# Attention masks kept in SBUF for all heads instead of being loaded for every score step

## The chip, the cores and the metric

One Trainium2 chip, all 8 NeuronCores, one launch, no exchange between the cores. The metric is the device time in microseconds of the slowest core.

## The reference, cut to what matters

One transformer layer: x is [2, 4096, 2048]; causal attention with 16 query heads and 4 key/value heads of 128, then a feed-forward part with LoRA experts.

```python
x = x + attn(_layernorm(x))        # scores = q k^T / sqrt(128); masked where key > query; softmax; @ v; @ wo
x = x + ffn(_layernorm(x))         # silu(x W1) * (x W3) with rank-32 experts, top 2 of 8, then W2
```

## The kernel before

Each core owns 1024 query rows of one sequence. It works in four stages, each engine's instructions being queued in program order, with semaphores between the engines.

Stage A (L255 to L413) normalises the sequence of 4096 rows and the core's own 1024 in tiles of 256, and projects K and V, which stay in SBUF. Then a short pass squares K (into `sq_t`) and finds its largest norm on the DVE (L411 to L453).

Stage C goes over the 16 heads (L465 to L652). A head starts with its Q projection (32 matmuls, L473), then a norm bound for the softmax (L488 to L536, small operations on four engines in turn). Then come 32 steps over blocks of 128 keys. Step `sx` emits its scores, `emit_sc`, and behind them `emit_lav` of step `sx-2` (row sums by a column of ones, L598 and L601, and the product with V, L606 and L609). Steps 0 to 15 serve both halves of the queries (7 matmuls of 512 columns with those of `emit_lav`), steps 16 to 31 only the second (4 matmuls). The causal mask is added on TensorE: a matmul of -60 times the identity with a 128x512 mask tile (L556 in the first half, L566 in the second). ACT takes the exponentials (L582, L586). A head ends with two reciprocals, their broadcast (L632, L634) and the scaling of its output.

The mask tile of step `sx` lies in one of two buffers, `mk_sb[sx % 2]`, and is loaded anew in every step of every head, by the sync engine's queue. That queue waits until the scores of step `sx-2` are done, since they read the same buffer:

```python
P.wait('sync', 'pe', scg_s.get(sx - 2) or scg31_prev)
mdma = P.dma('sync', mk_sb[sx % 2], masks_h[:, sx * 512:(sx + 1) * 512], sem=f'dM{sx % 2}')
```

The score matmuls of step `sx` wait for it, in front of the first of them (L553 or L563), besides the exponential that frees their PSUM bank.

The output projection follows (16 tiles `oc`, L669): `wo_sb` by the GpSimd queue, after the last head, and the residual `xoc_sb` by the sync queue, in front of a DVE addition (L680); then two stores. `xoc_sb[0]` waits for nothing but the mask loads queued ahead of it. The feed-forward part D follows in two halves of 512 rows.

The areas of the stages overlap in SBUF: the working area of stage C starts where that of stage A starts, and `sq_t` of stage A ends up under `wo_sb`, `xoc_sb` and `ev_sb` of the output projection.

Of the kernel before, what the change touches and what calls it, by code (L numbers as in the profile page):

```python
# [11 lines left out]
BF16 = mybir.dt.bfloat16  # L12
# [84 lines left out]
def build_program():  # L97
    nc = bass.Bass('TRN2', target_bir_lowering=False)

    def din(name, shape, dtype=F32):  # L100
        return nc.dram_tensor(name, list(shape), dtype, kind='ExternalInput').ap()
# [12 lines left out]
    masks_h = din('masks_h', [128, 32 * 512], BF16)  # L114
# [27 lines left out]
    with es:  # L142
# [17 lines left out]
        WC = Arena(nc, SB_WORK, SB_GLB, 'wc')  # L160
# [5 lines left out]
        mk_sb = [WC.al(f'mk{i}', [128, 512], BF16) for i in range(2)]  # L166
        recA = WC.al('recA', [1, 512], F32)
        recB = WC.al('recB', [1, 512], F32)
        wo_sb = [WC.al(f'wo{i}', [128, NCH * 128], BF16) for i in range(2)]
        xoc_sb = [WC.al(f'xoc{i}', [128, TOWN], F32) for i in range(2)]  # L170
        ev_sb = [WC.al(f'ev{i}', [128, TOWN], F32) for i in range(2)]

        WD = Arena(nc, SB_WORK, SB_GLB, 'wd')
        w13 = [WD.al(f'w13_{i}', [128, 2 * NCH * 128], BF16) for i in range(2)]
# [31 lines left out]
        nbi_sb = GLB.al('nbi', [128, 128], BF16)  # L206
# [22 lines left out]
        P = _P(sems)  # L229
# [25 lines left out]
        for i in range(NT + 2):  # L255
# [12 lines left out]
            if have:  # L268
                lnb = pb[4 + (i % 2)]
                wts = [(f'dX{i % 2}', ms['xb'][i]), ('dC1', d_c1)]  # L270
# [10 lines left out]
            if 0 <= j < NT:  # L281
                lnb = pb[4 + (j % 2)]
                wts = [('pe', ms['sumsq'][j])]
# [21 lines left out]
            if have:  # L305
                wts = [(f'dX{i % 2}', ms['xb'][i])]
# [14 lines left out]
            if 0 <= j < NT:  # L321
                bcb = pb[6 + (j % 2)]
                wts = [('ve', ms['post'][j])]
# [20 lines left out]
            if 0 <= j < NT:  # L344
# [4 lines left out]
                wts = [('ve', ms['rbb'][j])]  # L349
# [21 lines left out]
            if 0 <= jj < NTA:  # L371
# [19 lines left out]
                wts = [('ve', ms['ap'][jj]), ('dWkv', d_wkv)]  # L391
# [20 lines left out]
        a_pe, a_sc, a_ve = P.cnt['pe'], P.cnt['sc'], P.cnt['ve']  # L412
# [38 lines left out]
            ], waits=[('ve', kb_ve)], inc='ve')  # L451
        kb_done = kb_ve
        kb_pe_done = kb_pe_last  # L453

        P.wait('gpsimd', 've', a_ve)
        P.wait('gpsimd', 'pe', a_pe)
# [2 lines left out]
        scg31_prev = None  # L459
# [3 lines left out]
        for h in range(NH):  # L463
# [15 lines left out]
            wts = [(f'dQ{h % 2}', qdma)]  # L479
# [57 lines left out]
            exp_s, lav_s, scg_s = {}, {}, {}  # L537

            def emit_sc(sx):
                rot = sx % 2  # L540
                pi = sx % 4
                bA = pb[2] if rot == 0 else pb[0]
                bB = (pb[3] if rot == 0 else pb[1]) if sx < 16 else pb[sx % 4]
                ksl = slice(kv * S + sx * 128, kv * S + (sx + 1) * 128)
                if h == 0 and sx == 0:
                    P.wait('sync', 've', a_ve)
                    P.wait('sync', 'pe', a_pe)
                P.wait('sync', 'pe', scg_s.get(sx - 2) or scg31_prev)
                mdma = P.dma('sync', mk_sb[sx % 2], masks_h[:, sx * 512:(sx + 1) * 512],
                             sem=f'dM{sx % 2}')  # L550
                scms = []
                if sx < 16:
                    scms.append((lambda ksl=ksl, h=h, bA=bA: (lambda e: e.matmul(  # L553
                        bA[:, 0:512], K_sb[:, ksl], q_sb[h % 2][:, 0:512],
                        start=True, stop=False, skip_group_check=True)))())
                    scms.append((lambda sx=sx, bA=bA: (lambda e: e.matmul(  # L556
                        bA[:, 0:512], nbi_sb, mk_sb[sx % 2],
                        start=False, stop=True, skip_group_check=True)))())
                    scms.append((lambda ksl=ksl, h=h, bB=bB: (lambda e: e.matmul(  # L559
                        bB[:, 0:512], K_sb[:, ksl], q_sb[h % 2][:, 512:1024],  # L560
                        start=True, stop=True, skip_group_check=True)))())
                else:
                    scms.append((lambda ksl=ksl, h=h, bB=bB: (lambda e: e.matmul(  # L563
                        bB[:, 0:512], K_sb[:, ksl], q_sb[h % 2][:, 512:1024],
                        start=True, stop=False, skip_group_check=True)))())
                    scms.append((lambda sx=sx, bB=bB: (lambda e: e.matmul(  # L566
                        bB[:, 0:512], nbi_sb, mk_sb[sx % 2],
                        start=False, stop=True, skip_group_check=True)))())
                wts = [(f'dM{sx % 2}', mdma)]
                if sx <= 1:  # L570
                    wts += [('ve', qev), ('ve', vnbc)]
                elif sx < 16:
                    wts.append(('sc', exp_s[sx - 2]))
                elif sx < 20:
                    wts.append(('sc', exp_s[15]))
                else:
                    wts.append(('sc', exp_s[sx - 4]))
                scg_s[sx] = P.g('tensor', scms, waits=wts, inc='pe')

                exps = []  # L580
                if sx < 16:
                    exps.append((lambda rot=rot, pi=pi: (lambda e: e.activation(  # L582
                        out=p_sb[pi][:, 0:1024], in_=pq[1 - rot][:, 0:1024], func=AF.Exp,
                        bias=sml[:, 0:1])))())
                else:
                    exps.append((lambda pi=pi, bB=bB: (lambda e: e.activation(  # L586
                        out=p_sb[pi][:, 512:1024], in_=bB[:, 0:512], func=AF.Exp,
                        bias=sml[:, 0:1])))())
                pv = lav_s.get(sx - 4) or lav_prev4.get(sx - 4 + 32)
                exp_s[sx] = P.g('scalar', exps,  # L590
                                waits=[('pe', scg_s[sx]), ('ve', vnbc)] + ([('pe', pv)] if pv else []),
                                inc='sc')
# [24 lines left out]
            for sx in range(32):  # L617
                emit_sc(sx)
                if sx >= 2:
                    emit_lav(sx - 2)  # L620
# [27 lines left out]
            scg31_prev = scg_s[31]  # L648
            lav_prev4 = {k: lav_s[k] for k in (28, 29, 30, 31)}

        c_heads_pe = P.cnt['pe']
# [3 lines left out]
        for oc in range(NCH):  # L655
            if oc < 2:
                P.wait('gpsimd', 'pe', c_heads_pe)
            else:
                P.wait('gpsimd', 've', oc_ve[oc - 2])
            wodma = P.dma('gpsimd', wo_sb[oc % 2], wo_h[oc], sem=f'dO{oc % 2}')  # L660
            if oc >= 2:
                P.wait('sync', 've', oc_ve[oc - 2])
            xocdma = P.dma('sync', xoc_sb[oc % 2], xo_oc[oc], sem=f'dXoc{oc % 2}')

            oms = []
            for half in range(2):
                for hc2 in range(NCH):
                    def mk_o(half=half, hc2=hc2, oc=oc):
                        return lambda e: e.matmul(  # L669
                            pb[2 * (oc % 2) + half][:, 0:512],  # L670
                            wo_sb[oc % 2][:, hc2 * 128:(hc2 + 1) * 128],
                            acat[:, hc2 * TOWN + half * 512: hc2 * TOWN + (half + 1) * 512],
                            start=(hc2 == 0), stop=(hc2 == NCH - 1), skip_group_check=True)
                    oms.append(mk_o())
            wts = [(f'dO{oc % 2}', wodma), ('ve', evac_prev)]
            if oc >= 2:
                wts.append(('ve', oc_ve[oc - 2]))
            pe_oc = P.g('tensor', oms, waits=wts, inc='pe')
            oc_ve[oc] = P.g('vector', [
                (lambda half, oc=oc: (lambda e: e.scalar_tensor_tensor(  # L680
                    ev_sb[oc % 2][:, half * 512:(half + 1) * 512],
                    pb[2 * (oc % 2) + half][:, 0:512], bo_sb[:, oc:oc + 1],
                    xoc_sb[oc % 2][:, half * 512:(half + 1) * 512],
                    op0=ALU.add, op1=ALU.add)))(half)
                for half in range(2)
            ], waits=[('pe', pe_oc), (f'dXoc{oc % 2}', xocdma),
                      (f'dSt{oc % 2}', oc_st[oc - 2] if oc >= 2 else 0)], inc='ve')
            P.wait('sync', 've', oc_ve[oc])
            for tt in range(2):
                v = P.dma('sync', xres_d[tt, :, oc, :], ev_sb[oc % 2][:, tt * TD:(tt + 1) * TD],  # L690
                          sem=f'dSt{oc % 2}')
            oc_st[oc] = v
# [10 lines left out]
        for tt in range(2):  # L703
            P.wait('sync', 'dSt0', xres_st0)
            P.wait('sync', 'dSt1', xres_st1)
            if prev_dn_ve:
                P.wait('sync', 've', prev_dn_ve)
            xr_dma = P.dma('sync', xrt.rearrange('p (c n) -> p c n', c=NCH), xres_d[tt],
                           sem='dXr')
# [24 lines left out]
            wts = [('ve', vcast)]  # L734
# [95 lines left out]
            for ts in range(4):  # L830
# [12 lines left out]
                wts = [('dXr', xr_dma), ('ve', dnm), ('ve', dse_v)]  # L843
# [76 lines left out]
            for mi, dstbuf in ((0, mer[0]), (1, mer[1]), (2, wmer[0]), (3, wmer[1])):  # L920
                for eh in range(2):
                    wts = [('ve', ts_ve)]
# [207 lines left out]
            for hc in range(NCH):  # L1130
                qpe = None
                for q in range(4):
# [17 lines left out]
                    wts = [(('dW0', 'dW1', 'dW2')[idx % 3], w2dma), ('ve', x2ve[NFC - 1])]  # L1150
                    if q == 0 and hc >= 2:
# [8 lines left out]
                wts = [('pe', pedn), ('dXr', xr_dma),  # L1160
                       (f'oS{hc % 2}', last_st[hc % 2])]
# [130 lines left out]
```

How the kernel before makes its waits and increments, by code:

```python
        def run(e, dst=dst, src=src, s=s):  # L69
            e.dma_start(out=dst, in_=src).then_inc(s, 16)
# [3 lines left out]
    def wait(self, eng, sem, v):  # L74
        if not v:
            return
        s = self.sems[sem]
        self.streams[eng].append(lambda e, s=s, v=v: e.wait_ge(s, v))
# [6 lines left out]
        def run(e, builders=tuple(builders), ws=ws, inc=inc, incn=incn):  # L85
            for sname, v in ws:
                e.wait_ge(sems[sname], v)
            last = None
            for f in builders:
                last = f(e)
            if inc is not None:
                last.then_inc(sems[inc], incn)
# [1081 lines left out]
        @blk.sync  # L1174
        def _(e):
            for f in P.streams['sync']:
                f(e)
            e.wait_ge(sems['oS0'], n_out0)
            e.wait_ge(sems['oS1'], n_out1)
```

## Time and profile before

| what | value |
|---|---|
| median of 3 runs | 4073.96 us (4065.46 to 4077.08) |
| the profiled execution's own time | 4082.54 us |
| its span on the slowest core, core 4 | 4080.5 us |
| spans of the 8 cores | 4044.1 to 4080.5 us |
| TensorE busy, share of the span | 80% |
| head 8 on core 4, Q projection to the next head's | 81.9 us |
| mask loads | 512 of 128 KB |

The profile is of one execution. Rows name engine, line, operation and tiles: PE is TensorE, SPq the sync engine's DMA queue, POOL GpSimd. The ends of matmuls are modelled: in a dense stream they start 0.21 to 0.22 us apart while each is shown with 0.38 us, so an idle gap as the profile gives it is shorter than the time lost between the starts.

### The profile page before, as it was taken

The numbers are of one execution on the slowest core, as the hardware profiler recorded it, in microseconds if no ns is written. First come the engines' busy times: TensorE is split into PE (matmuls) and PEld (weight loads), VectorE is DVE, ScalarE is ACT, GpSimd is POOL, SyncE is SP. The second block draws the span as 40 slices with busy tenths as digits, with TensorE's granted clock in tenths as the row PEclk, the third lists the DMA queues.
The fourth block names the chain that finished last, engine by engine and source line by source line (L and its number), as shares of the span: only waits on it lengthen the run. The fifth ranks groups of instructions, "written<-read, shape, count | busy, mean of one in ns | idle before, by whom it ended". The sixth has DMA issues, their size and how long they took to land.

```text
span 4080.5 us, 39777 instructions; the slowest of 8 cores (4044.1 to 4080.5 us)
## 1 busy us (share of the span) xinstructions
PE 3257.8 (80%) x13863; PEld 1386.0 (34%) x14108; DVE 840.0 (21%) x1355; ACT 732.3 (18%) x882; POOL 292.5 (7%) x556
## 2 busy tenths in 40 slices
PE   5887737777777778777745999998894599999898
PEld 3454412222222222222314444443331344444333
DVE  2333341111111211111122122222001222222200
ACT  1111124333343334332000101110000001111000
POOL 0000000000000000000000111111110011111111
PEclk7778858888888888888975999999997599999999
DMA  5121212221222122212650777665894166666588
GB/s 97 31 42 32 42 30 60 63 58 49 59 59 64 51 56 62 61 49 57 164 138 9 116 122 122 119 122 93 139 154 97 26 122 124 121 121 118 95 150 142
DMA packets 166528, 350.15 MB, mean 86 GB/s; under 512 B 19259, under 2 KB 99396, under 8 KB 162500
## 3 DMA queue, kind: packets, MB, share of 16 engines
q0 software_dynamic: 79488, 246.45, 35.8%
q1 hardware_dynamic: 86852, 101.15, 8.0%
q8 instruction: 123, 2.02, 0.2%
q14 instruction: 65, 0.53, 0.0%
HBM read 577.17 MB, written 16.78 MB: 146 GB/s over the span
## 4 chain that ended last, share of the span: by engine, by line
PE 66%; DMA 15%; DVE 10%; issue 4%; ACT 4%; another core or an unknown queue 0%; SPq 0%; DVEq 0%; ACTq 0%; POOL 0%; POOLq 0%
PE pq L991 9%; PE pq L1002 9%; PE pq L1145 5%; DMA wd_w2s<-w_h 5%; DMA wc_mk<-masks_h 3%; PE pq L376 3%; PE pq L473 3%; PE pq L385 3%; DMA wc_xoc<-xo_oc 2%; PE pq L609 2%; PE pq L601 2%; PE pq L598 2%; PE pq L606 2%; PE pq L563 2%; PE pq L553 2%
## 5 line engine op out<-in xcount | busy, mean ns | idle before, releaser
L1145 PE MATMUL pq<-dp_x2s,wd_w2s 128*128 128x512 bf16 x1756 | 403.2, 382 | 60.1 <-DMA wd_w2s<-w_h 57.4
L991 PE MATMUL pq<-wd_xln,wd_w 128*128 128x512 bf16 x1756 | 407.7, 383 | 45.0 <-DMA wd_b<-b_h 39.5
L1002 PE MATMUL pq<-wd_xln,wd_w 128*128 128x512 bf16 x1752 | 402.0, 379 | 2.1
L582 ACT ACTIVATE wc_p<-pq,gl_sml 128x1024 bf16<-128x1024 f32 x256 | 284.9, 1113 | 216.6 <-PE pq L559 214.8
L1145 PEld LDWEIGHTS pq<-dp_x2s,wd_w2s 128*128 128x128 bf16 x1792 | 171.4, 98 | 288.9 <-issue 98.0
L991 PEld LDWEIGHTS pq<-wd_xln,wd_w 128*128 128x128 bf16 x1792 | 176.2, 99 | 260.2 <-issue 54.1
L1043 ACT ACTIVATE dp_s<-pq 128x512 bf16<-128x512 f32 x112 | 66.9, 597 | 1031.8 <-PE pq L1036 1009.7
L1070 DVE TENSOR_TENSOR dp_x<-dp_s,pq 128x512 bf16<-128x512 bf16 x112 | 77.1, 688 | 835.5 <-PE pq L1062 827.7
L1002 PEld LDWEIGHTS pq<-wd_xln,wd_w 128*128 128x128 bf16 x1792 | 175.4, 98 | 211.4
L625 DVE RECIPROCAL wc_recA<-pq 1x512 f32<-1x512 f32 x16 | 53.5, 3346 | 886.8 <-PE pq L609 886.8
L586 ACT ACTIVATE wc_p<-pq,gl_sml 128x512 bf16<-128x512 f32 x256 | 175.9, 687 | 212.3 <-PE pq L566 204.4
L70 POOL DMA_DIRECT2D wd_w<-w_h x224 | 118.9, 537 | 1202.1 <-PE pq L1005 878.9
L601 PE MATMUL pq<-wc_p,gl_ocb 128*1 128x512 bf16 x512 | 197.2, 385 | 1.2
L609 PE MATMUL pq<-wc_p,pp_V 128*128 128x512 bf16 x491 | 192.7, 393 | 2.9 <-issue 2.4
L669 PE MATMUL pq<-pp_acat,wc_wo 128*128 128x512 bf16 x502 | 123.4, 406 | 40.0 <-DMA wc_wo<-wo_h 39.5
L563 PE MATMUL pq<-wc_q,pp_K 128*128 128x512 bf16 x252 | 94.9, 377 | 72.5 <-DMA wc_mk<-masks_h 41.2
L473 PE MATMUL pq<-pp_xlnown,wc_wq 128*128 128x512 bf16 x501 | 142.4, 451 | 5.8 <-DVE gl_cms L450 4.8
L553 PE MATMUL pq<-wc_q,pp_K 128*128 128x512 bf16 x253 | 108.6, 429 | 25.8 <-DMA wc_mk<-masks_h 17.7
L376 PE MATMUL pq<-wa_xln,wkv_wk 128*128 128x256 bf16 x1024 | 128.6, 292 | 0.0
L632 PE MATMUL pq<-wc_recA,gl_orf 1*128 1x512 f32 x32 | 32.6, 1121 | 115.1 <-DVE wc_recB L628 115.1
L385 PE MATMUL pq<-wkv_wv,wa_xln 128*128 128x512 bf16 x496 | 117.8, 399 | 1.1
L376 PEld LDWEIGHTS pq<-wa_xln,wkv_wk 128*128 128x128 bf16 x1024 | 105.7, 105 | 24.9 <-issue 6.7
(180 smaller groups left out, 3360.0 us busy)
## 6 DMA issues: line engine op xcount, KB each, us to landing
wd_w<-w_h POOLq DMA_DIRECT2D x224, 512.0 KB, 7.3
wc_mk<-masks_h SPq DMA_DIRECT2D x512, 128.0 KB, 2.0
wd_w2s<-w_h POOLq DMA_DIRECT2D x128, 448.0 KB, 6.3
wa_xb<-x_tiles POOLq DMA_DIRECT2D x16, 1024.0 KB, 9.2
wd_b<-b_h POOLq DMA_DIRECT2D x112, 128.0 KB, 7.6
wc_wq<-wq_h POOLq DMA_DIRECT2D x16, 512.0 KB, 5.3
wc_xoc<-xo_oc SPq DMA_DIRECT2D x16, 512.0 KB, 7.1
wc_wo<-wo_h POOLq DMA_DIRECT2D x16, 512.0 KB, 7.4
```

The source lines that it names most:

```text
L376: return lambda e: e.matmul(pb[kv // 2][:, (kv % 2) * TA:(kv % 2 + 1) * TA], wk_sb[:, hc * 512 + kv * 128: hc * 512 + (kv + 1) * 128], xln ...
L385: return lambda e: e.matmul(pb[2 + sub][:, 0:512], xln_t[jj % 2][:, hc * TA + sub * 128: hc * TA + (sub + 1) * 128], wv_sb[:, hc * 512:(hc ...
L473: return lambda e: e.matmul(pq[0][:, half * 512:(half + 1) * 512], wq_sb[h % 2][:, hc * 128:(hc + 1) * 128], xlnown[:, hc * TOWN + half * ...
L553: scms.append((lambda ksl=ksl, h=h, bA=bA: (lambda e: e.matmul(bA[:, 0:512], K_sb[:, ksl], q_sb[h % 2][:, 0:512], start=True, stop=False, ...
L563: scms.append((lambda ksl=ksl, h=h, bB=bB: (lambda e: e.matmul(bB[:, 0:512], K_sb[:, ksl], q_sb[h % 2][:, 512:1024], start=True, stop=Fals ...
L582: exps.append((lambda rot=rot, pi=pi: (lambda e: e.activation(out=p_sb[pi][:, 0:1024], in_=pq[1 - rot][:, 0:1024], func=AF.Exp, bias=sml[: ...
L586: exps.append((lambda pi=pi, bB=bB: (lambda e: e.activation(out=p_sb[pi][:, 512:1024], in_=bB[:, 0:512], func=AF.Exp, bias=sml[:, 0:1])))())
L601: lav.append((lambda pi=pi, sx=sx: (lambda e: e.matmul(pb[5][0:1, 0:512], ocb_sb, p_sb[pi][:, 512:1024], start=(sx == 0), stop=(sx == 31), ...
L609: lav.append((lambda pi=pi, vsl=vsl, sx=sx: (lambda e: e.matmul(pb[7][:, 0:512], V_sb[:, vsl], p_sb[pi][:, 512:1024], start=(sx == 0), sto ...
L991: x1ms = [(lambda hc, bx1=bx1, w=lw13: (lambda e: e.matmul(bx1[:, 0:TD], w(hc, 0), xln2[:, hc * TD:(hc + 1) * TD], start=(hc == 0), stop=F ...
L1002: x3ms = [(lambda hc, bx3=bx3, w=lw13: (lambda e: e.matmul(bx3[:, 0:TD], w(hc, 1), xln2[:, hc * TD:(hc + 1) * TD], start=(hc == 0), stop=F ...
L1145: return lambda e: e.matmul(pb[hc % 2][:, 0:TD], w2s[idx % 3][:, jj * 128:(jj + 1) * 128], x2s[:, fc2 * TD:(fc2 + 1) * TD], start=(q == 0 ...
```

## The change

All 32 mask tiles are loaded once, as one tensor `mkall` of 128 x 16384 bf16 (4 MB), and stay in SBUF for all heads. `mkall` lies where `wo_sb`, `xoc_sb` and `ev_sb` come to lie later, and where `sq_t` was. So its one load waits until the last matmul that reads `sq_t` is done, and the first score step of the first head waits for the load. The two loads of `xoc_sb` that formerly waited for no buffer now wait until the heads are done. `mk_sb` stays allocated and is not used.

```diff
+        mko = WC.off
         wo_sb = [WC.al(f'wo{i}', [128, NCH * 128], BF16) for i in range(2)]
         xoc_sb = [WC.al(f'xoc{i}', [128, TOWN], F32) for i in range(2)]
         ev_sb = [WC.al(f'ev{i}', [128, TOWN], F32) for i in range(2)]
+        WCM = Arena(nc, mko, 216064, 'wcm')
+        mkall = WCM.al('mkall', [128, 32 * 512], BF16)
...
         kb_pe_done = kb_pe_last
+        P.wait('sync', 'pe', kb_pe_done)
+        P.wait('sync', 've', a_ve)
+        d_mk = P.dma('sync', mkall, masks_h, sem='dM0')
...
-                if h == 0 and sx == 0:
-                    P.wait('sync', 've', a_ve)
-                    P.wait('sync', 'pe', a_pe)
-                P.wait('sync', 'pe', scg_s.get(sx - 2) or scg31_prev)
-                mdma = P.dma('sync', mk_sb[sx % 2], masks_h[:, sx * 512:(sx + 1) * 512],
-                             sem=f'dM{sx % 2}')
...
-                        bA[:, 0:512], nbi_sb, mk_sb[sx % 2],
+                        bA[:, 0:512], nbi_sb, mkall[:, sx * 512:(sx + 1) * 512],
...
-                wts = [(f'dM{sx % 2}', mdma)]
+                wts = []
+                if h == 0 and sx == 0:
+                    wts.append(('dM0', d_mk))
...
             if oc >= 2:
                 P.wait('sync', 've', oc_ve[oc - 2])
+            else:
+                P.wait('sync', 'pe', c_heads_pe)
             xocdma = P.dma('sync', xoc_sb[oc % 2], xo_oc[oc], sem=f'dXoc{oc % 2}')
```

## Rows read from the trace of the kernel before

**Rows 1.** Busy time of the engines, whole span: us (share) xinstructions.
```profile
PE 3257.8 (80%) x13863; PEld 1386.0 (34%) x14108; DVE 840.0 (21%) x1355; ACT 732.3 (18%) x882; POOL 292.5 (7%) x556
```

**Rows 2.** Groups by line: operation, tiles, count | busy us, mean ns | idle before, releasers.
```profile
L553 PE MATMUL pq<-wc_q,pp_K 128*128 128x512 bf16 x253 | 108.6, 429 | 25.8 <-DMA wc_mk<-masks_h 17.7 <-DVE gl_sml L534 7.1 <-ACT wc_p L582 0.3
L563 PE MATMUL pq<-wc_q,pp_K 128*128 128x512 bf16 x252 | 94.9, 377 | 72.5 <-DMA wc_mk<-masks_h 41.2 <-ACT wc_p L586 19.8 <-ACT wc_p L582 6.9
L566 PE MATMUL pq<-wc_mk,gl_nbi 128*128 128x512 bf16 x246 | 92.9, 377 | 3.1 <-DMA wc_mk<-masks_h 1.9 <-ACT wc_p L586 1.2
```

**Rows 3.** Windows: steps 16 to 31 of the 16 heads; stretch, length, busy by engine, clock, DMA.
```profile
639.30:664.20 24.90, 20.62 (x70) 5.35 (x72) 0.00 (x0) 10.99 (x16) 0.00 (x0) 1.00 0.28 84
...
sum 400.20, PE 329.81 PEld 85.26 DVE 0.00 ACT 175.91 POOL 0.00; mean PE 20.61 PEld 5.33 DVE 0.00 ACT 10.99 POOL 0.00
```

**Rows 4.** Timeline of TensorE, first head, steps 16 to 31: start us, length, instruction, idle before.
```profile
648.33 0.38 PE L563 MATMUL pq<-wc_q,pp_K 128*128 128x512 bf16 x1 [0.34 <-ACT wc_p L586]
...
649.83 0.38 PE L563 MATMUL pq<-wc_q,pp_K 128*128 128x512 bf16 x1 [0.28 <-ACT wc_p L586]
...
657.79 0.38 PE L563 MATMUL pq<-wc_q,pp_K 128*128 128x512 bf16 x1 [0.84 <-DMA wc_mk<-masks_h]
...
658.84 0.38 PE L563 MATMUL pq<-wc_q,pp_K 128*128 128x512 bf16 x1
...
659.68 0.39 PE L609 MATMUL pq<-wc_p,pp_V 128*128 128x512 bf16 x1
...
661.73 0.38 PE L563 MATMUL pq<-wc_q,pp_K 128*128 128x512 bf16 x1
...
663.82 0.39 PE L609 MATMUL pq<-wc_p,pp_V 128*128 128x512 bf16 x1
```

**Rows 5.** DMA issues: tiles, queue, count, KB each, median us from issue to landing.
```profile
wc_mk<-masks_h SPq DMA_DIRECT2D x512, 128.0 KB, 2.0
```

**Rows 6.** Timeline of ACT, the same head.
```profile
659.64 0.69 ACT L586 ACTIVATE wc_p<-pq,gl_sml 128x512 bf16<-128x512 f32 x1 [0.37 <-PE pq L566]
```

**Rows 7.** Timeline of TensorE and ACT, first steps of head 8.
```profile
1277.26 0.63 PE L559 MATMUL pq<-wc_q,pp_K 128*128 128x512 bf16 x1
1278.91 0.58 PE L553 MATMUL pq<-wc_q,pp_K 128*128 128x512 bf16 x1 [1.02 <-DMA wc_mk<-masks_h]
...
1276.82 1.11 ACT L582 ACTIVATE wc_p<-pq,gl_sml 128x1024 bf16<-128x1024 f32 x1 [3.06 <-PE pq L559]
```

**Rows 8.** Timeline of TensorE from the last matmuls on `sq_t` to the first scores.
```profile
585.00 1.86 PE L426 MATMUL pq<-wa_sq,gl_ocb 128*1 128x512 bf16 x4 [3.34 <-DVE gl_krow L447]
...
608.95 0.58 PE L553 MATMUL pq<-wc_q,pp_K 128*128 128x512 bf16 x1 [0.41 <-DVE gl_sml L534]
```

**Rows 9.** Tile view of `xrt`: its two loads of 4096 KB on the sync queue.
```profile
DMA to landing us min/median/max: 20.9/25.6/30.3
```

**Rows 10.** From the last head to the output projection: timeline, chain, tile view, DMA issues.
```profile
1902.74 0.42 SPq L70 DMA_DIRECT2D wc_xoc<-xo_oc  x1
...
1918.90 6.36 DMA wc_wo<-wo_h
...
L680 DVE SCALAR_TENSOR_TENSOR wc_ev<-pq,gl_bo,wc_xoc x32: 741/746/751, 1935.4 to 2082.6; 128x512 f32<-128x512 f32 x32
...
wc_wo<-wo_h POOLq DMA_DIRECT2D x16, 512.0 KB, 7.4
```

**Rows 11.** Windows of stage A, of head 8 and of part D (columns as in rows 3).
```profile
119.00:138.00 19.00, 17.05 (x97) 10.05 (x96) 3.77 (x9) 0.00 (x0) 0.00 (x0) 0.81 0.31 56
...
1282.40:1328.80 46.40, 41.50 (x157) 11.36 (x158) 0.00 (x0) 25.30 (x29) 0.00 (x0) 1.00 0.26 77
2260.00:2800.00 540.00, 533.62 (x2426) 242.11 (x2475) 131.55 (x256) 55.34 (x102) 89.61 (x169) 1.00 0.71 121
```

**Rows 12.** The chain in order of time, V projection of two tiles: start, us, what.
```profile
125.63 8.33 PE pq L385 x31
...
330.19 6.87 PE pq L385 x31
```

More of the change, by code:

```diff
@@ L566, in emit_sc @@
                     scms.append((lambda sx=sx, bB=bB: (lambda e: e.matmul(
-                        bB[:, 0:512], nbi_sb, mk_sb[sx % 2],
+                        bB[:, 0:512], nbi_sb, mkall[:, sx * 512:(sx + 1) * 512],
                         start=False, stop=True, skip_group_check=True)))())
-                wts = [(f'dM{sx % 2}', mdma)]
+                wts = []
+                if h == 0 and sx == 0:
+                    wts.append(('dM0', d_mk))
                 if sx <= 1:
```

## The prediction

> **What bounds the kernel now.** I read the page first: TensorE is busy 80% of the span [rows 1] and no other engine comes near, so the question is what TensorE waits for in the stage that the change touches. The view by line answers for the score matmuls: the first matmul of a step sat idle for the mask load 17.7 us in steps 0 to 15 (17 times, about once a head) and 41.2 us in steps 16 to 31, and the mask matmul of those steps for 1.9 us [rows 2]. That is 60.8 us shown. A further 19.8 us stand under ACT L586 and 6.9 us under L582 [rows 2].
>
> Idle time shown is not yet time lost, because matmul ends are modelled. So I measured starts instead, in windows cut at the first L563 and the last L609 of each head: the second halves take 400.20 us in the 16 heads, 25.01 us each [rows 3]. Within them the timeline shows two paces. A slow step runs from 648.33 to 649.83, 1.50 us; a fast one from 657.79 to 658.84, 1.05 us [rows 4], and the fast one holds the same four matmuls. 1.05 us is the pace of TensorE itself: from 658.84 the last of the four starts 0.84 us later, at 659.68 [rows 4], and one more distance of about 0.21 us ends the step.
>
> What makes 1.50? Sync may reload a buffer only when the scores that read it are done, two steps earlier. The round takes 0.21 + 0.38 us from the start of L563 to the modelled end of L566, plus 2.0 us from issue to landing [rows 5]: 2.59 us, and some 0.4 us of hand-overs on both sides make 3.0 us for two steps, thus 1.50 a step. The alternating fast steps and stalls late in the first head (0.84 us of idle before 657.79, then none before 658.84) [rows 4] are the same loop in another rhythm. The 19.8 us under ACT I read as the mask too. The exponential that L563 needs is that of four steps earlier, long over: ACT starts 0.80 us after its step's L563 (659.64 against 658.84) and runs 0.69 us [rows 6], so it is done 1.49 us after it, and its PSUM bank is wanted four steps, at least 4.2 us, after it.
>
> In steps 0 to 15 the reload has seven matmuls to hide behind and is late only at step 2.
>
> **Part by part: steps 16 to 31.** All 512 loads and their waits go. What is late next? `emit_lav` of a step wants that step's exponential, two steps on: at the fast pace it comes 2 x 1.05 + 2 x 0.22 = 2.54 us after the scores and the exponential is ready at 1.49 us. ACT needs 0.69 us and a short gap of 0.37 us or less [rows 6] per 1.05 us. So TensorE's own pace holds. The half then takes 15 intervals and a tail: two intervals carry the two extra matmuls of `emit_lav` 14 and 15 (1.05 + 2 x 0.22 = 1.49, say 1.5 us), thirteen take 1.05, and from the last L563 at 661.73 to the last L609 at 663.82 plus 0.38 are 2.47 us [rows 4]. Together 3.0 + 13.65 + 2.47 = 19.1 us; 16 x 19.1 = 306 us against 400.2: **94 us gained**.
>
> **Steps 0 to 15.** Step 2 of head 8 starts at 1278.91 and would start, without the load, when its exponential is over, 1276.82 + 1.11 = 1277.93, so about 0.9 us sooner [rows 7]; the 17.7 us of [rows 2] say 1.1 us a head. There the matmuls run slowly, 0.63 us long [rows 7] against 0.38 [rows 4], which is the 1.2 GHz level. If the return to 2.4 GHz comes at the same moment whatever was done before it, work brought forward is worth about half of its time. Bounds 9 and 17.7 us; I take the middle, **13 us**.
>
> **The one load of 4 MB.** It may start when the last matmuls on `sq_t` are done, 585.00 + 1.86 = 586.9 us, and is wanted at 608.95 [rows 8]: 22 us. Queued ahead of it on sync are only the constants, long landed; nothing on sync stands behind it until the heads are over, since the mask loads were all that sync did there. The nearest rows are the loads of `xrt`: 4096 KB, the same queue, the same contiguous 32 KB a partition, all cores at once. They landed in 20.9 and 30.3 us, both while GpSimd loaded weights [rows 9]. Here GpSimd has nothing to load beside it: the Q weights of heads 0 and 1 wait for stage A alone and are long in, those of head 2 wait for head 0's Q projection. So the load should land sooner than 20.9 us, by 608 at the latest: **0 us**, bounded by 30.3: 586.9 + 30.3 = 617.2, 8.3 us late, paid once. If it were still later, TensorE would queue behind the first scores with everything after them.
>
> The Trainium skill, "DMA: Bandwidth & Descriptors", section on the anatomy of one DMA, gives a fit of 2.0 us plus bytes over 436 GB/s, for the GpSimd path; by it the estimate would be 11.6 us, landing near 599. No run so far shows such a load undisturbed.
>
> **Loads after the heads.** `xoc` 0 was issued at 1902.74, inside the last head, and now goes together with the first two `wo` at 1918.90. The DVE wants it at 1935.4 only [rows 10], so its own lateness is hidden. But the first `wo`, on which TensorE waits, landed in 6.36 us without that neighbour, and in 7.4 us in the median of the stage, where each has one [rows 10]: **1 us lost**, 0 to 2. The wait on `xoc` 1 costs nothing: in queue order it already follows the DVE's first result.
>
> **Nothing else moves.** Addresses and matmul sizes stay, PSUM banks and the four `p` buffers too. The Q projection, the norm bound and the reciprocals at a head's ends remain as they are. Less DMA traffic in the heads helps the Q weights, which nothing waits for.
>
> **Sum.** 94 + 13 - 0 - 1 = 106 us. Against the profiled execution's own 4082.5 us this makes 3976.5. That execution lies 8.5 us above the median of the runs, 4074; from the median the forecast is **3968 us**, 2.6% less. A difference of more than 0.3%, about 12 us, is what a measurement of this kernel can tell from none.
>
> **Rivals.**
>
> 1. *Another chain paces steps 16 to 31.* For it speaks that the profile names ACT for 19.8 + 6.9 us of the idle time [rows 2]. If those waits are real, only the waits named for the mask go: 60.8 - 1 = 60 us, 4014 us. Against it speak the exponential that is ready 1 us early, worked out above, and the fast steps that did happen.
>
> 2. *The first load is late.* Priced above at up to 8.3 us: 3976 us. For it, 8 cores fetch 4 MB each at once; against it, the `xrt` loads did that too.
>
> 3. *The clock falls on denser work, and the kernel gets slower.* In part D the granted clock is 1.00 with TensorE busy 533.62 of 540 us, and in the dense part of head 8 it is 1.00, but in stage A core 4 was granted 0.81 from 119 to 138 us [rows 11]. There 31 V matmuls took 8.33 us, against 6.87 us later [rows 12], 21% more. After the change a head has its dense stretch of 46.4 us [rows 11] less the 6 us gained, and 32 matmuls of Q projection at 0.22 us, 7 us, at the full level: some 47.5 us; 21% of that is 10 us a head, 160 us in all, and 106 us of gain would become a loss of 54: 4128 us. It decides once the lower clock covers 106 / 16 / 0.21 = 32 us of a head, on one die alone, since the slowest core counts. Against it: part D is denser than the heads can become and keeps 1.00.
> The Trainium skill, "TensorE: Matmul & The Clock Gate", Part 1, states a peak-current limit that takes a die to 13/16 of the clock once three of its cores run dense matmuls. The 0.81 in stage A agrees with it; the 1.00 in part D, which every core runs, does not.
>
> 4. *The change does nothing that counts:* the load is not what L563 waits for, and both halves stay as they are. 4074 us. Only a wrong reading of every releaser would bring this.
>
> **How the numbers follow.** The forecast 0.79, rival 1 0.11, rival 2 at its full price 0.03, rival 3 0.05, rival 4 0.02. The forecast's own spread: 94 could be 98 or 88 by the pace at the seams, 13 is 9 to 17.7, the load 0 to 8.3, `wo` 0 to 2; how long the 1.2 GHz stretch at a head's start lasts may change with the head's length, and two matmuls more or fewer in it, 0.25 us each, are 16 x 0.5 = 8 us; the runs of before lie within 12 us. From 3968 that reaches from 3945 to 3990. Rival 1 in a mild form (a pace of 1.15 us, 13 x 0.1 x 16 = 21 us lost) lies at 3989, so I extend the upper end to 4000 and leave out the full rival 1, rivals 3 and 4. Faster 0.93 (forecast, rivals 1 and 2), same 0.02 (rival 4), slower 0.05 (rival 3).
>
> **What would show it.** Idle of L553 and L563 with the mask load as releaser gone; the second half of a head 19.1 us; steps of 1.05 us; idle under ACT L586 gone with it (if it stays, rival 1). Step 2 some 0.9 us sooner. One 4 MB load issued near 587 us that lands before the first L553, whose idle stays 0.4 us. The first `wo` landing in about 7.4 us. Granted clock 1.00 in the second halves; 0.81 there would be rival 3. Lengths of stage A and part D unchanged. The prediction is wrong if the steps do not fall below about 1.2 us, or if the clock does.

## The result, and the profile after

The changed kernel takes 3946.6 us in the median of 9 runs, against 4071.7 us for the kernel before (10 runs): 125 us less. The ratio is 0.9695, with a 95% interval of 0.9677 to 0.9712. The forecast was 3968 us, so the direction and most of the size were right and the gain came out about 20 us larger than the likeliest value; the time lies 1.6 us above the lower end of the range, 3945 us. Several chips had executions in which one die ran at a lower clock; the comparisons leave them out, and where few others remained I read the lengths of stages on cores whose clock was undisturbed.

The slowest core of the profiled execution is now core 0, with a span of 3946.0 us. First the page, busy time of the engines:

```profile
PE 3221.9 (82%) x14108; PEld 1377.2 (35%) x14108; DVE 839.5 (21%) x1355; ACT 732.8 (19%) x882; POOL 292.7 (7%) x556
```

The groups by line, the score matmuls and the mask matmul of the second half:

```profile
L553 PE MATMUL pq<-wc_q,pp_K 128*128 128x512 bf16 x256 | 107.7, 421 | 10.5 <-DVE gl_sml L540 7.6 <-ACT wc_p L584 2.8
L563 PE MATMUL pq<-wc_q,pp_K 128*128 128x512 bf16 x256 | 97.0, 379 | 6.5 <-ACT wc_p L584 6.5
L566 PE MATMUL pq<-wcm_mkall,gl_nbi 128*128 128x512 bf16 x256 | 97.0, 379 | 0.0
```

No idle time under the mask load is left. In front of L563, 72.5 us [rows 2] have become 6.5 us. The 19.8 us that stood under the exponentials of steps 16 to 31 are gone with the mask's, as the prediction read them; the 6.9 us under those of steps 0 to 15 are real and stayed, as 6.5 us: once a head, step 16 waits for the exponential of step 15.

Windows of steps 16 to 31 of the 16 heads, on core 0 of the changed kernel, first head and sum:

```profile
622.41:641.64 19.23, 19.23 (x72) 5.18 (x72) 0.00 (x0) 11.01 (x16) 0.00 (x0) 1.00 0.00 1
...
sum 307.88, PE 307.80 PEld 82.90 DVE 0.00 ACT 176.05 POOL 0.00; mean PE 19.24 PEld 5.18 DVE 0.00 ACT 11.00 POOL 0.00
```

TensorE is busy in all 19.23 us of such a stretch, the granted clock is 1.00, and the sum is 307.9 us where core 4 had 400.2 [rows 3]. The timeline of TensorE inside one shows the step:

```profile
631.75 0.38 PE L563 MATMUL pq<-wc_q,pp_K 128*128 128x512 bf16 x1
631.97 0.38 PE L566 MATMUL pq<-wcm_mkall,gl_nbi 128*128 128x512 bf16 x1
632.28 0.38 PE L603 MATMUL pq<-wc_p,gl_ocb 128*1 128x512 bf16 x1
632.59 0.39 PE L611 MATMUL pq<-wc_p,pp_V 128*128 128x512 bf16 x1
632.81 0.38 PE L563 MATMUL pq<-wc_q,pp_K 128*128 128x512 bf16 x1
```

From 631.75 to 632.81 are 1.06 us, the fast pace of [rows 4], now in every step.

The round that set the slower pace can be read directly from the chain of the kernel before, core 4:

```profile
655.48 2.07 DMA wc_mk<-masks_h
657.54 0.24 issue
657.79 0.38 PE pq L563
658.16 0.23 PE pq L566
658.45 1.98 DMA wc_mk<-masks_h
```

One reload begins at 655.48 and the next of the chain at 658.45: 2.97 us for a load, the start of the step and the two matmuls that read the mask, which is what the prediction had put together as 3.0 us.

To compare a core with itself, the two sums of steps 0 to 15 over the 16 heads, on core 0. Before:

```profile
sum 481.99, PE 457.35 PEld 123.37 DVE 0.00 ACT 284.94 POOL 0.00; mean PE 28.58 PEld 7.71 DVE 0.00 ACT 17.81 POOL 0.00
```

After:

```profile
sum 448.71, PE 439.31 PEld 121.85 DVE 0.00 ACT 285.18 POOL 0.00; mean PE 27.46 PEld 7.62 DVE 0.00 ACT 17.82 POOL 0.00
```

This is 33.3 us less, where the prediction had 13. The start of head 8 shows what else changed. The timeline of TensorE on core 0 before:

```profile
1262.25 0.59 PE L553 MATMUL pq<-wc_q,pp_K 128*128 128x512 bf16 x1 [0.48 <-DVE gl_sml L534]
...
1266.18 0.59 PE L553 MATMUL pq<-wc_q,pp_K 128*128 128x512 bf16 x1 [1.21 <-DMA wc_mk<-masks_h]
...
1268.90 0.59 PE L609 MATMUL pq<-wc_p,pp_V 128*128 128x512 bf16 x1
1269.33 0.38 PE L553 MATMUL pq<-wc_q,pp_K 128*128 128x512 bf16 x1
```

And after:

```profile
1195.30 0.59 PE L553 MATMUL pq<-wc_q,pp_K 128*128 128x512 bf16 x1 [0.48 <-DVE gl_sml L540]
...
1198.20 0.59 PE L553 MATMUL pq<-wc_q,pp_K 128*128 128x512 bf16 x1 [0.19 <-ACT wc_p L584]
...
1199.57 0.43 PE L600 MATMUL pq<-wc_p,gl_ocb 128*1 128x512 bf16 x1
1199.84 0.38 PE L603 MATMUL pq<-wc_p,gl_ocb 128*1 128x512 bf16 x1
```

Step 2 starts 2.90 us after step 0 instead of 3.93 us: the stall itself was worth 1.0 us. But the first matmul of 0.38 us, that is at 2.4 GHz, comes 4.5 us after the head's first score instead of 7.1 us. On average over the heads 9 matmuls are slow instead of 14. A slow one mostly starts 0.42 to 0.43 us after the one before it and a fast one 0.21 to 0.22 us, so 5 fewer slow ones are the second microsecond of each head.

Not every head of the kernel before paid it. Of its 128 heads (16 on each of 8 cores) 124 had 12 to 18 slow matmuls, but head 4 on cores 3, 5, 6 and 7 had 6: there the stall came as well, and the first matmul behind it was already fast. In the changed kernel all 128 heads had 8 to 10.

The one load of 4 MB, with the last matmuls on `sq_t` and the first scores (sync queue and TensorE timelines, then the tile view):

```profile
569.92 1.86 PE L429 MATMUL pq<-wa_sq,gl_ocb 128*1 128x512 bf16 x4 [3.33 <-DVE gl_krow L450]
...
571.92 0.33 SPq L70 DMA_DIRECT2D wcm_mkall<-masks_h  x1
...
594.21 0.58 PE L553 MATMUL pq<-wc_q,pp_K 128*128 128x512 bf16 x1 [0.41 <-DVE gl_sml L540]
...
DMA to landing us min/median/max: 16.0/16.0/16.0
```

It landed at 587.9, 6.3 us before it was wanted, and in 13.4 to 16.0 us on the eight cores. The row of [rows 9] was a bound on the safe side, and the estimate by the Trainium skill ("DMA: Bandwidth & Descriptors", anatomy of one DMA, 11.6 us) is 1.8 to 4.4 us short of these. Its fit is for the GpSimd path; this load went by the sync queue, on eight cores at once. Which of the two makes the difference no run shows.

After the heads, the chain of the changed kernel has:

```profile
1779.69 6.80 DMA wc_wo<-wo_h
1786.49 0.24 issue
1786.73 8.78 PE pq L673 x32
```

The first `wo` took 6.80 us beside `xoc` 0. Core 4's 6.36 us before [rows 10] is not the value to compare with: core 0 itself had 5.12 us, and the median of the eight cores went from 5.1 to 6.7 us. So about 1.6 us were lost.

### The profile page after: what moved, and what is told of

It reads as the page before. It is cut to its first block, busy times and chain, and to the rows that moved or that the text cites. A ratio compares the mean times of both kernels' runs of the same rounds, so it can differ in the third digit from the quotient of the medians.

```text
span 3946.0 us, 38492 instructions; the slowest of 8 cores (3922.9 to 3946.0 us)
## 1 busy us (share of the span) xinstructions
PE 3221.9 (82%) x14108; PEld 1377.2 (35%) x14108; DVE 839.5 (21%) x1355; ACT 732.8 (19%) x882; POOL 292.7 (7%) x556
## 4 chain that ended last, share of the span: by engine, by line
PE 71%; DMA 11%; DVE 10%; ACT 4%; issue 3%; SPq 0%; DVEq 0%; POOL 0%; ACTq 0%; POOLq 0%
PE pq L995 10%; PE pq L1006 10%; PE pq L1149 6%; DMA wd_w2s<-w_h 5%; PE pq L479 4%; PE pq L611 3%; PE pq L603 3%; PE pq L379 3%; PE pq L388 3%; DMA wc_xoc<-xo_oc 2%; PE pq L608 2%; PE pq L600 2%; PE pq L553 2%; PE pq L340 2%; PE pq L559 2%
## 5 line engine op out<-in xcount | busy, mean ns | idle before, releaser
L1167 DVE TENSOR_TENSOR gl_dn<-pq,dp_xrt 128x512 f32<-128x512 f32 x32 | 22.1, 691 | 449.5 <-PE pq L1159 449.5
L553 PE MATMUL pq<-wc_q,pp_K 128*128 128x512 bf16 x256 | 107.7, 421 | 10.5 <-DVE gl_sml L540 7.6
```

## The experiments

The table gives, for each kernel on one core, the mean over the 16 heads of five lengths, all taken between starts in the timeline of TensorE: Q projection to the matmuls of the norm bound, from there to the first score, steps 0 to 15, steps 16 to 31 (to the last matmul plus 0.38 us); then all heads from the first Q matmul to the last product with V. "Slow" is the number of matmuls over 0.55 us long in steps 0 to 15.

| kernel, core | Q | norm | steps 0-15 | steps 16-31 | slow | heads | ratio to the kernel before |
|---|---|---|---|---|---|---|---|
| before, 0 | 12.23 | 4.89 | 30.12 | 25.30 | 14.2 | 1323.4 | 1 |
| changed, 0 | 12.29 | 4.76 | 28.04 | 19.24 | 9.0 | 1192.0 | 0.9695 (0.9677 to 0.9712) |
| second half resident, 3 | 12.92 | 5.13 | 30.43 | 19.24 | 15.2 | 1246.0 | 0.987 (0.981 to 0.993) |
| first half resident, 2 | 12.72 | 5.10 | 28.09 | 25.01 | 9.2 | 1297.4 | 0.998 (0.994 to 1.003) |
| four buffers, 5 | 12.28 | 4.76 | 28.04 | 19.29 | 9.0 | 1192.5 | 0.975 (0.969 to 0.980) |
| reload at step 2, 7 | 12.97 | 5.12 | 30.31 | 19.24 | 15.1 | 1245.0 | 0.985 (0.978 to 0.992) |
| norm gap filled, 3 | 12.22 | 4.50 | 26.75 | 19.24 | 0 | 1166.0 | 0.961 (0.951 to 0.971) |
| both gaps filled, 3 | 11.60 | 4.50 | 26.75 | 19.24 | 0 | 1129.2 | 0.9507 (0.9488 to 0.9526), second timing |

My theory: two waits on the reload round cost, each by itself, and the traffic costs nothing. The rival: 64 MB of loads and 512 DMA issues slow the stage. The intervals of the ratios are up to 2% wide and many overlap, so the lengths of the heads decide, and the ratio only has to agree with them.

**Only the second half resident.** Steps 0 to 15 reload into two buffers as before.

```diff
+                rotm = sx < 16
+                if rotm:
+                    P.wait('sync', 'pe', scg_s.get(sx - 2) or scg31_prev)
+                    mdma = P.dma('sync', mk_sb[sx % 2], masks_h[:, sx * 512:(sx + 1) * 512],
+                                 sem=f'dM{sx % 2}')
+                mrow = mk_sb[sx % 2] if rotm else mkall[:, sx * 512:(sx + 1) * 512]
```

> Masks of steps 16 to 31 resident, those of steps 0 to 15 reloaded into two buffers as before. Theory (each wait on the reload round costs by itself, traffic costs nothing): steps 16 to 31 take 19.2 us a head as in the changed kernel, steps 0 to 15 keep their 30.0 to 30.2, so 16 x 2.0 = 32 us above the changed kernel's 3947: 3979 us. Rival (the 512 loads slow the rest by their traffic): half of the loads remain, so about half of the gain goes, near 4010 us, and steps 16 to 31 come out between 19.2 and 25.

Steps 16 to 31 keep the whole of their gain, 19.24 us a head, though half of the loads still run. The heads take 54 us more than in the changed kernel, not 32: steps 0 to 15 account for 38, as the sum of their windows shows (486.83 against 448.71), and 16 come from the Q projection (0.63 us a head) and the norm bound (0.37). By the heads the ratio should be 0.983, and the measured 0.987 (0.981 to 0.993) agrees; the expected 3979 us would be 0.977.

```profile
sum 486.83, PE 461.50 PEld 123.69 DVE 0.00 ACT 285.32 POOL 0.00; mean PE 28.84 PEld 7.73 DVE 0.00 ACT 17.83 POOL 0.00
```

**Only the first half resident.**

```diff
-                rotm = sx < 16
+                rotm = sx >= 16
```

> The mirror image: masks of steps 0 to 15 resident, those of steps 16 to 31 reloaded into two buffers. Theory: steps 0 to 15 take 28.1 us a head, steps 16 to 31 25.0 to 25.3, so 16 x 5.9 = 95 us above 3947: 4042 us, and the losses of the two mirror images add up to the whole difference of 125 us. Rival (traffic, or one half's wait shifting into the other): they add up to clearly more or less, and this one too lies near 4010.

The two halves are separate: 28.09 and 25.01 us. The windows of steps 16 to 31:

```profile
sum 400.14, PE 336.78 PEld 85.55 DVE 0.00 ACT 175.91 POOL 0.00; mean PE 21.05 PEld 5.35 DVE 0.00 ACT 10.99 POOL 0.00
```

The heads take 105 us more than in the changed kernel: 92 in these steps (400.1 less 307.9) and 12 again in the Q projection and the norm bound. So the losses of the mirror images, 54 + 105 = 159 us, are more than the 131 us by which the heads of core 0 shrank. The expectation that they add up failed (the ratio, expected 0.993, would be 0.995 by the heads; 0.994 to 1.003 was measured), through the parts of a head that neither touches: its first 17 us take 17.8 to 18.1 us in both mirror images and 17.1 in both full kernels.

**Four rotating buffers.** The kernel before with every load kept, but four steps to make it in.

```diff
-        mk_sb = [WC.al(f'mk{i}', [128, 512], BF16) for i in range(2)]
+        mk_sb = [WC.al(f'mk{i}', [128, 512], BF16) for i in range(4)]
...
-                P.wait('sync', 'pe', scg_s.get(sx - 2) or scg31_prev)
+                P.wait('sync', 'pe', scg_s.get(sx - 4) or scg_prev4.get(sx + 28))
```

> The kernel before, with four mask buffers instead of two: all 512 loads and all their traffic stay, but a reload has four steps to be made in. Theory (the round of about 3.0 us is the whole cost): four steps at 1.05 us are 4.2 us, longer than the round, and steps 0 to 3 of a head find their masks ready, so all waits go: 28.1 and 19.2 us a head, 3947 us within 10. Rival (traffic or queue load of 512 DMAs costs): part of the gain is missing, above 3970 us.

The lengths of the heads are those of the changed kernel, 1192.5 us, with all the traffic. Windows of steps 16 to 31, first head and sum:

```profile
617.52:636.75 19.23, 19.23 (x72) 5.18 (x72) 0.00 (x0) 11.01 (x16) 0.00 (x0) 1.00 0.38 111
...
sum 308.67, PE 308.24 PEld 83.06 DVE 0.00 ACT 176.01 POOL 0.00; mean PE 19.27 PEld 5.19 DVE 0.00 ACT 11.00 POOL 0.00
```

The DMA engines are busy for 0.38 of the time and move 111 GB/s, where the changed kernel moves next to nothing, and the half takes 19.23 us in both. This refutes the rival: the round was the cost, the traffic was not. I timed it a second time:

> The kernel with four rotating mask buffers once more for its time, for the same reason. Its undisturbed cores spanned 3929 to 3945 us and its heads 1192.0 us, as long as in the changed kernel: 3947 us, within 10.

The second ratio is 0.972 (0.969 to 0.975). Its interval overlaps that of the changed kernel; whether a difference of about 0.3% remains, the times don't say, but the heads show none.

**One reload a head, at step 2.**

```diff
+                rotm = sx == 2
+                if rotm:
+                    P.wait('sync', 'pe', scg_s[0])
+                    mdma = P.dma('sync', mk_sb[0], masks_h[:, 1024:1536], sem='dM0')
+                mrow = mk_sb[0] if rotm else mkall[:, sx * 512:(sx + 1) * 512]
```

> The changed kernel, but in each head the mask of step 2 alone is loaded again after the scores of step 0: one wait a head is put back. Theory (the stall of about 1 us at step 2 also delays TensorE's return to 2.4 GHz by a few matmuls): steps 0 to 15 take 30.0 us instead of 28.1, 14 slow matmuls instead of 9, 3947 + 32 = 3978 us. Rival (the stall costs its own 0.95 us only, and the other 1 us a head came from elsewhere in steps 0 to 15): 29.0 us, still 9 slow matmuls, 3962 us.

One stall of about 1 us a head brings back the whole loss of steps 0 to 15: 30.31 us and 15 slow matmuls. Their windows:

```profile
sum 485.03, PE 460.64 PEld 124.93 DVE 0.00 ACT 284.93 POOL 0.00; mean PE 28.79 PEld 7.81 DVE 0.00 ACT 17.81 POOL 0.00
```

That is 36.3 us more than the changed kernel's 448.7, where 16 stalls of about 1 us explain 16. The rival of the expectation, that a stall costs only itself, is refuted. The length of a head does not explain the slow matmuls either: without the stall there are 9, in heads that last 75.2 us (changed) and 81.7 us (first half resident); with it there are 14 to 15, in heads of 83.4 us (before) and 78.5 us (this kernel and the second half resident). Its heads are 53 us longer, against 54 with all reloads of steps 0 to 15 put back: step 2 is the only place where they mattered.

> The kernel with one reload a head, at step 2, once more for its time, since in the first timing most of its runs were on disturbed cores. Its undisturbed cores spanned 3975 to 3985 us, with 3.3 us a head above the changed kernel; expected 3946 + 53 = 3999 us by the heads' span, or 3978 by those cores.

The repetition gave 0.982 (0.977 to 0.988), and 3999 over 4072 is 0.982.

**The gaps in front of the first score filled.** If idle TensorE in front of a head's scores is what lowers their clock, work without use should raise it.

```diff
+            P.g('tensor', [
+                (lambda k: (lambda e: e.matmul(
+                    pb[2][:, 0:512], K_sb[:, k * 128:(k + 1) * 128], V_sb[:, 0:512],
+                    start=True, stop=True, skip_group_check=True)))(k)
+                for k in range(12)
+            ], waits=[('ve', evac_prev)])
             pe_qs = P.g('tensor', [
```

and the same 12 in front of the matmul that broadcasts the norm bound.

> The changed kernel with 24 matmuls added per head, whose results nobody reads: 12 between the Q projection and the matmuls of the norm bound, 12 behind these, where TensorE stood idle for 3 us each. Theory (the clock at a head's start is low because TensorE was idle before it, and each of the 9 slow matmuls costs 0.21 us): steps 0 to 15 start at 2.4 GHz and take about 26.5 us instead of 28.1, the added matmuls hide in the gaps: 3947 - 25 = 3922 us, between 3912 and 3935. Rival (the low clock does not depend on it, or the added matmuls delay the norm bound): nothing gained or slower, 3947 to 3990 us.

The timeline of TensorE on core 3 (the added matmuls are L508 and L542):

```profile
1170.25 2.75 PE L508 MATMUL pq<-pp_V,pp_K 128*128 128x512 bf16 x12
1173.50 0.38 PE L514 MATMUL pq<-wc_csq,gl_ocb 128*1 128x512 bf16 x1 [0.50 <-ACT wc_csq L502]
...
1174.02 2.76 PE L542 MATMUL pq<-pp_V,pp_K 128*128 128x512 bf16 x12
...
1177.97 0.38 PE L565 MATMUL pq<-wc_q,pp_K 128*128 128x512 bf16 x1 [0.48 <-DVE gl_sml L552]
```

The first score matmul takes 0.38 us, none is slow, and steps 0 to 15 take 26.75 us. The heads are 26 us shorter, as expected; the ratio, 0.961 (0.951 to 0.971), overlaps that of the changed kernel and could not have told this alone. So the low clock in steps 0 to 15 does come from the idle time ahead of them.

**The gap of the reciprocals filled too**, with 28 such matmuls a head.

```diff
+            P.g('tensor', [
+                (lambda k: (lambda e: e.matmul(
+                    pb[0][:, 0:512], K_sb[:, k * 128:(k + 1) * 128], V_sb[:, 0:512],
+                    start=True, stop=True, skip_group_check=True)))(k)
+                for k in range(28)
+            ], waits=[('sc', exp_s[31])])
             perb = P.g('tensor', [
```

> As the kernel with the gaps of the norm bound filled, and 28 more matmuls without use behind the last product with V, where TensorE waits 7.2 us for the two reciprocals: 52 a head. Theory: the Q projection starts at 2.4 GHz too and takes about 1.5 us less a head, and the broadcast matmuls of the reciprocals are faster: 16 x 2 = 32 us more gained, 3890 us. Rival (52 added matmuls a head draw the granted clock down to 0.81 somewhere, or are in the way): slower than the one with fewer.

The heads take 1129.2 us, 63 less than in the changed kernel: the Q part is 0.7 us shorter than in the changed kernel, and from the broadcast to the next Q projection are 1.88 us instead of 3.68. A second timing gave its ratio:

> The kernel with both gaps of a head filled, without the reordered residual loads, once more for its ratio: its heads spanned 1129 us in the trace, 63 less than in the changed kernel, so 3946 - 63 = 3883 us and a ratio to the kernel before of 0.954. If the disturbance of most of its first runs belonged to the kernel and not to the chip, it returns here and the ratio stays above 0.96.

It took 3880.8 us in the median, 0.9507 (0.9488 to 0.9526) of the kernel before. The 63 us of the heads would make 0.954; where the rest comes from, the stages don't show. The clock did not fall: the mean granted clock over the span is 0.919 to 0.925 of full speed on the eight cores, against 0.890 to 0.894 in the changed kernel, and over the heads alone it is 0.98 (core 3) against 0.88 (core 0). For comparison, the heads had 0.86 in the kernel before (core 0) and 0.83 with one reload at step 2 (core 7).

**Residual loads one tile ahead.** In the changed kernel the DVE waits for `xoc` 118.8 us in all.

```diff
+            if oc == 0:
+                P.wait('sync', 'pe', c_heads_pe)
+                xocd = [P.dma('sync', xoc_sb[k], xo_oc[k], sem=f'dXoc{k}') for k in range(2)]
...
             P.wait('sync', 've', oc_ve[oc])
+            if oc + 2 < NCH:
+                xocd.append(P.dma('sync', xoc_sb[oc % 2], xo_oc[oc + 2], sem=f'dXoc{oc % 2}'))
```

> The changed kernel with the residual loads of the output projection issued one tile ahead: a buffer is reloaded as soon as the DVE has read it, ahead of the stores, and the first two go together. In the changed kernel the DVE waits 118.8 us for these loads in all, 14 times. Theory: the period of a tile falls from 9.9 to about 8 us, where the weight load that waits for the result of two tiles before takes over: 14 x 1.9 = 27 us less, 3920 us. Rival (the weight load, longer beside two neighbours, takes the whole of it): 3940 us or more.

The wait went: no idle time of the DVE under `xoc` is left, and it now waits for TensorE alone. But another wait took its place. The chain on core 7:

```profile
1799.94 8.24 DMA wc_wo<-wo_h
1808.18 0.35 issue
1808.53 8.77 PE pq L672 x32
...
1819.48 7.85 DMA wc_wo<-wo_h
```

From one of these weight loads to the next are 19.5 us, for two tiles: weight load, 32 matmuls and result of one behind the other. That is as long as before (the chain of the changed kernel has a result every 9.4 to 10.0 us, at 1795.69, 1805.09, 1814.70 and 1824.69), and so core 7 shows the rival. It is the worst of the eight, though. From the last product of the heads to the last matmul of the stage are 166.3 to 172.9 us on six cores and 176.4 and 179.8 us on cores 3 and 7, against 173.7 to 176.3 us in the changed kernel. So most cores gained some 5 us and core 7, the slowest of this execution, lost 3.5; the 27 us of the theory came on none. The ratio, 0.966 (0.962 to 0.970), can't be told from the changed kernel's.

**The load of the masks late.** It waits for the first Q projection.

```diff
+            if h == 0:
+                P.wait('sync', 'pe', pe_q)
+                P.wait('sync', 've', a_ve)
+                d_mk = P.dma('sync', mkall, masks_h, sem='dM0')
```

> The changed kernel, but the one load of 4 MB waits until the Q projection of the first head is done. It landed in 16.0 us on the slowest core and 13.4 to 16.0 on all, so it is now wanted some 8 us before it lands. Theory (late once, nothing behind it, paid in full): first scores 7 to 10 us later, idle of that length in front of the first L553, plus up to 1.5 us for the clock: 3947 + 9 = 3956 us. Rival (TensorE catches up elsewhere, or the loss multiplies): 3947 or above 3970.

Core 5, timeline of TensorE:

```profile
604.76 0.59 PE L554 MATMUL pq<-wc_q,pp_K 128*128 128x512 bf16 x1 [11.21 <-DMA wcm_mkall<-masks_h]
```

The load, issued at 586.4, landed 18.0 us later, the first score came 10.4 us later than it would have, and the heads took 1199.9 us, 8 more. The ratio is 0.970, and its interval (0.965 to 0.975) is too wide to show 8 us. A late load is paid once and not multiplied: 8 of the 10.4 us here, 10 on core 1.

**All together:** the edits of the last kernels but the late load, gaps filled and residual loads ahead, which need no lines beyond those shown.

> The changed kernel with both gaps filled by matmuls without use and the residual loads one tile ahead. The three parts touch different stretches, so the savings seen one by one on undisturbed cores should add: the heads 1129 us instead of 1192 (63 us), the output projection 6 us: 3946 - 69 = 3877 us, ratio to the kernel before about 0.952. If the added matmuls cost the rest of the kernel its clock: above 3890.

The heads took 1129 us again, as expected, and the ratio was 0.954 (0.949 to 0.959), expected 0.952. The 6 us expected from the output projection did not come: from the last product to its last matmul are 171.7 to 178.2 us on the eight cores, against 170.3 to 175.1 in the kernel with filled gaps alone. It does not beat that kernel, and whether the reordered loads harm there stays open.

## Why the prediction was right, and where it was off

- *Steps 16 to 31: 94 us, from 1.50 to 1.05 us a step.* Right. They gained 92.3 us against core 4's 400.2, 97.0 against core 0's own 404.9; a head's half takes 19.24 us, forecast 19.1. The 0.4 us of hand-overs in the round was a remainder that made the sum fit 1.50 us; the chain has 2.97 us for the whole round and bears it out. The reading of the ACT releaser as the mask was right for the 19.8 us.
- *Steps 0 to 15: 13 us, bounded by 9 and 17.7.* The wait at step 2 and its length were read rightly, and this term was mis-sized: it measured 32 us against core 4 (480.4 us there) and 33 on core 0. The step that failed is "if the return to 2.4 GHz comes at the same moment whatever was done before it". It came 2.5 us sooner in head 8, and 5 matmuls sooner on average, so both bounds were too low: they priced the stall and left out what the stall did to the clock. The kernel with one reload a head shows it: one wait of 1 us costs 2.3 us there, and 1 us more in the Q projection and the norm bound. That the time still lies in the stated range is partly luck: for this stretch the range allowed 5 us beyond the 13, and 8 us for two slow matmuls more or fewer, and the term missed by 20.
- *The one load: 0 us.* Right, with 6.3 us to spare.
- *The first `wo`: 1 us.* About 1.6 us in the median of the cores, 1.7 on core 0, inside the stated 0 to 2; the 6.36 us of core 4, from which it was worked out, was higher than on six of the other cores (5.1 to 5.3 us).
- *Nothing else moves.* Nearly. On core 0 the heads gained 131.4 us and the span 123.6; what lies ahead of the heads was 2.0 us longer, and what lies behind them 5.8 us. The latter differs as much from core to core: 2160 to 2181 us before.
- *Rival 1*, another chain at 4014 us, and *rival 4*, no effect, are refuted by the steps of 1.06 us. *Rival 2*: the load was not late, and made late it cost about what the prediction said, its delay once. *Rival 3*, the granted clock at 0.81, did not appear on any core of the changed kernel's profile, nor with 52 more matmuls a head. In the kernel with the second half resident cores 4 and 5 had it until about 60 us into the heads, and not after. The prediction took the 0.81 in stage A as agreeing with the peak-current limit of the Trainium skill ("TensorE: Matmul & The Clock Gate", Part 1), by which a whole die falls to 13/16. Only the level agrees: from 119 to 138 us cores 4 and 5 had 0.81 and 0.80, while cores 6 and 7 of the same die had 0.89 and 0.93. In part D of the kernel before, from 2260 to 2800 us, all eight cores were granted 1.00 with TensorE busy 534 to 540 us; there the measurement goes against the page, and it decides.

Sum by the measured terms, core 0 against itself: 97.0 + 33.3 in the steps and 1 in the rest of the heads are 131.4 us; less 2.0 and 5.8 they make the 123.6 us of its span, and the medians differ by 125 us.

Open: the Q projection and the norm bound are 0.8 to 1.0 us a head longer in the kernels whose heads last 78.5 or 81.7 us than in those with 75.2 or 83.4. I take it that the head's length decides how many of their matmuls meet the low clock, but I did not vary the length alone. Open too is why the clock came back during the stall in four of the 128 heads before and behind it in all others; no run moves the stall against the start of the head.

## What to carry to other kernels

Look at the start-to-start pace of a loop, not at its idle time: 61 us were shown under the load, 125 us came back. A buffer that is reloaded after its reader is done can't be used again before the reader's time and the load's whole round trip are over, here 3.0 us, however idle the DMA engines are; with two buffers that sets the pace of two steps. A second pair of buffers cured it as well as keeping all data resident. And a stall in a stretch at the low clock should be priced with what it does to the clock, here as much again as the stall.

## What the runs showed of the hardware that I had not expected

A stall of 1.0 us among slow matmuls put off their return to 2.4 GHz by 2.5 us in head 8, from 4.5 to 7.1 us behind the head's first score, and in 124 of 128 heads it was put off in this way. And 52 matmuls a head that compute nothing of use make the kernel 1.9% faster than the changed one (0.9507 against 0.9695; 1.6% by the length of the heads), by keeping TensorE at 2.4 GHz across gaps of 3 to 7 us: the granted clock over the heads is 0.98 instead of 0.88.
